# A fused Mamba and gated-FFN kernel: one more product on GpSimd, the layer norm's sums on ScalarE, and two changed instruction orders

## The reference, cut to what matters

```python
def layer(x):                                   # x: (4, 2048, 256)
    x = layernorm(x + mamba(x))
    return layernorm(x + ffn(x))

def mamba(h):                                   # 512 inner channels d, 16 states n
    x, z = split(h @ in_proj.T)
    u = silu(causal_conv4(x) + conv_b)
    dt_lo, B, C = split(u @ x_proj.T)           # 64, 16, 16 columns
    delta = softplus(dt_lo @ dt_proj.T + dt_b)
    A = -exp(A_log)
    # for each t:  h[d,n] = exp(delta[t,d]*A[d,n]) * h[d,n] + (delta[t,d]*u[t,d]) * B[t,n]
    #              y[t,d] = sum_n h[d,n] * C[t,n]
    return ((y + u * D) * silu(z)) @ out_proj.T

def ffn(x):                                     # ternary weights, hidden 1024
    h = silu(x @ w1.T * s1) * (x @ w2.T * s2)
    h = gelu(h @ h1.T * sh1); h = gelu(h @ h2.T * sh2)
    return h @ w3.T * s3
```

## Time and profile before

| | us |
|---|---|
| median of 3 runs | 3083.61 (3081.98 to 3090.67) |
| the profiled execution | 3080.23, its span 3078.4 |
| first stage's 15 full tile periods, 138.72 to 1880.20 us of the span | 1741.48 |
| DVE busy in them | 1679.70 |
| POOL busy in them | 1561.22 |
| ACT busy in them | 1322.19 |
| PE busy in them | 1512.33, at a mean granted clock of 0.92 |

### The profile page before, as it was taken

One profiled execution on the slowest core, in us unless ns is written; L12 is line 12 of the kernel. 1 busy time (PEld: TensorE's weight loads), 2 busy tenths in 40 slices (PEclk: granted clock), 3 DMA queues, 4 the chain that ended last, 5 costly groups with the idle time before them and its releaser, 6 DMA issues. The chain is left out here.

```text
span 3078.4 us, 40908 instructions
## 1 busy us (share of the span) xinstructions
PE 2735.4 (89%) x11540; PEld 1620.8 (53%) x11540; DVE 2331.5 (76%) x2785; ACT 2006.6 (65%) x3383; POOL 1705.2 (55%) x856
## 2 busy tenths in 40 slices
PE   5788998898898898888898886889999999999997
PEld 2243343343343343343343332678888888888886
DVE  5999999999999999999999999344444444444452
ACT  3777777777777777777777776555555455555442
POOL 3798898898898899898898898300000000000000
PEclk8799999999999899999999987999999999999999
DMA  7466466466476476475475466542222222222210
GB/s 254 96 186 164 124 192 169 120 192 168 120 192 164 121 196 164 117 199 152 129 198 154 127 192 204 187 146 95 69 75 89 68 82 84 79 68 89 75 42 15
DMA packets 239645, 412.04 MB, mean 134 GB/s; under 512 B 23264, under 2 KB 63456, under 8 KB 239456
## 3 DMA queue, kind: packets, MB, share of 16 engines
q1 hardware_dynamic: 175680, 297.67, 35.8%
q10 hardware_dynamic: 63776, 112.22, 11.1%
HBM read 285.55 MB, written 124.26 MB: 133 GB/s over the span
## 5 line engine op out<-in xcount | busy, mean ns | idle before, releaser
L1268 DVE TENSOR_TENSOR_SCAN h<-bank,state,db 128x512 f32<-128x512 f32 x1024 | 1252.2, 1270 | 52.8 <-POOL hc L1127 26.9
L1127 POOL TENSOR_TENSOR hc<-h,c_rows 128x1024 f32<-128x1024 f32 x512 | 1198.4, 2375 | 55.8 <-PE bank L660 41.5
L918 ACT ACTIVATE bank<-d_bc,a_neg 128x512 f32<-128x512 f32 x1024 | 691.8, 685 | 288.2 <-DVE h L1268 181.8
L1627 ACT ACTIVATE hring<-s_bank,sc 128x512 f32<-128x512 f32 x248 | 170.3, 687 | 488.6 <-PE s_bank L1560 488.3
L1560 PE MATMUL s_bank<-mid,h_r 128*128 128x512 f32 x2048 | 468.7, 390 | 4.6 <-DVEq L1654 4.6
L1252 DVE TENSOR_TENSOR db<-bank,du_bc 128x2048 f32<-128x2048 f32 x192 | 435.8, 2270 | 9.2 <-issue 7.4
L1560 PEld LDWEIGHTS s_bank<-mid,h_r 128*128 128x128 f32 x2048 | 385.7, 188 | 85.3 <-ACTq L1598 5.0
L732 PE MATMUL bank<-x_t,w 128*128 128x512 f32 x1088 | 366.0, 463 | 51.4 <-ACT ab L982 51.1
L1138 POOL TENSOR_TENSOR db<-du_bc,b_row 128x2048 f32<-128x2048 f32 x64 | 291.2, 4550 | 116.4 <-DVE h L1268 110.8
L633 PE MATMUL bank<-bc,w_spread 64*128 64x512 f32 x272 | 142.3, 533 | 203.3 <-DVE db L1252 201.3
L660 PE MATMUL bank<-hc,fold_w 128*32 128x512 f32 x2048 | 307.0, 675 | 9.1 <-DVE uz L1292 5.5
(11 more groups left out here) (145 smaller groups left out, 3706.5 us busy)
## 6 DMA issues: line engine op xcount, KB each, us to landing
ab<-ab ACTq DMA_DIRECT2D x272, 256.0 KB, 3.4
du_bc<-du_rows SPq DMA_DIRECT2D x256, 256.0 KB, 4.7
d_bc<-d_rows SPq DMA_DIRECT2D x256, 256.0 KB, 7.8
s_abr<-ab SPq DMA_DIRECT2D x120, 512.0 KB, 3.8
w<-w ACTq DMA_DIRECT2D x136, 256.0 KB, 3.4
d_rows<-sp_r SPq DMA_DIRECT2D x64, 256.0 KB, 2.1
du_rows<-sp_w SPq DMA_DIRECT2D x64, 256.0 KB, 2.2
x<-res SPq DMA_DIRECT2D x17, 512.0 KB, 9.0
```

Source lines behind the costliest of these rows:

```text
L918: act.activation(decays[DECAY_BANK[g]][:], d_bc[c % 2][:, j, :], ACT.Exp, scale=a_neg[:, g:g + 1]).then_inc(decay, 1)
L1127: pool.tensor_tensor(hc[:, k % HCSTEPS, at:at + HG], h[:, H_SLOT[k], at:at + HG], c_rows[:, q, :].unsqueeze(1).broadcast_to([P, HG, NT]), ...
L1268: dve.tensor_tensor_scan(h[:, H_SLOT[k], j, :], decays[DECAY_BANK[g]][:], db[:, k % DBSTEPS, j, :], state[:, g:g + 1], ALU.mult, ALU.add). ...
L1627: act.activation(hring[c % RING][:], p_h[m % HBANKS][:], ACT.Gelu, scale=sc[:, 2 + layer, m:m + 1]).then_inc(gelu, 1)
```

## The change

Five things are changed together.

1. **A fifth db on GpSimd.** Besides q = 3, step 10 (chunk 2, q = 2) goes to GpSimd. Steps 3, 7, 10, 11 and 15 are now GpSimd's, two of them in a row. VectorE's product and TensorE's spread for step 10 go away. Its rows of B come through one new spread at slot 13 into the softplus bank, and one new ScalarE copy at slot 14 into `b_row2`.
2. **Room for b_row2.** The ring of w1/w2 weights has three places in place of four.
3. **GpSimd's order.** The first half of hc now comes ahead of the db, the second half behind it.
4. **ScalarE's order.** A slot's decay now comes ahead of the DMA issue of that slot.
5. **The layer norm's sums.** bn_stats and bn_aggr leave VectorE. The four residual copies also write their row sums (`accum_out`), and ScalarE adds at slot 1 a 128x4 copy (the negative mean) and at slots 2 to 5 four Square activations with `accum_out`, written into the scratch `sp_e`. GpSimd's chain is one operation shorter.

```diff
+EXTRA_Q, EXTRA_C = 2, 2
+BY_POOL = [k % QN == QV or k == QN * EXTRA_C + EXTRA_Q for k in range(NK)]
+NPOOL = sum(BY_POOL)
...
+def pool_steps(k):
+
+    return k // NK * NPOOL + sum(BY_POOL[:k % NK])
...
-ABRING, W12RING = 3, 4
+ABRING, W12RING = 3, 3
@@ TensorE @@
-                        if exists(now) and g // JC % QN < QV:
+                        if exists(now) and not BY_POOL[g // JC]:
                             spread_b(now, g // JC)
...
+                        if i == ROW2_SLOT:
+                            pe.wait_ge(sp_dve, t.count(2 * KI, 2 * KI))
+                            spread_rows(p_dt, t, EXTRA_Q, row2_mm)
@@ ScalarE @@
-                act.activation(res[:, s, :], p_mm[s % 2][:, 0:DM], ACT.Copy).then_inc(out_sb, 1)
+                act.activation(res[:, s, :], p_mm[s % 2][:, 0:DM], ACT.Copy,
+                               accum_out=sums[:, s:s + 1]).then_inc(out_sb, 1)
...
+                if i == MEAN_SLOT:
+                    act.wait_ge(out_sb, t.count(SUB, OUT0))
+                    act.activation(mean4[:], sums[:], ACT.Copy, scale=-1.0 / DM).then_inc(ln_act, 1)
+                elif MEAN_SLOT < i <= MEAN_SLOT + SUB:
...
+                    act.activation(sp_e[:, s % 2 * DM:(s % 2 + 1) * DM], res[:, s, :], ACT.Square, bias=mean4[:, s:s + 1],
+                                   accum_out=squares[:, s:s + 1]).then_inc(ln_act, 1)
...
-                    if exists(t):
-                        ffn_stores(t, i)
                     now, g = at_group(t, n + EXP_LEAD)
                     if exists(now):
                         decay_of(now, g)
+                    if exists(t):
+                        ffn_stores(t, i)
...
+                        if i == ROW2_SLOT + 1:
+                            act.wait_ge(row2_mm, t.count(1, 1))
+                            act.wait_ge(db_pool, t.count(NPOOL, POOL0))
+                            act.activation(b_row2[:], p_dt[:], ACT.Copy).then_inc(row2_sb, 1)
@@ GpSimd @@
                     if n % JC == 0:
+                        done, at = at_group(t, n - JC)
+                        if exists(done):
+                            times_c(done, at // JC, range(1))
                         now, g = at_group(t, n + JC)
-                        if exists(now) and g // JC % QN == QV:
+                        if exists(now) and BY_POOL[g // JC]:
                             times_b(now, g // JC)
-                        now, g = at_group(t, n - JC)
-                        if exists(now):
-                            times_c(now, g // JC)
+                        if exists(done):
+                            times_c(done, at // JC, range(1, TURNS))
@@ VectorE @@
-                    if q < QV:
-                        dve.wait_ge(db_dve, t.count(KI * QV, QV * c + q + 1 + DVE0))
+                    if BY_POOL[k]:
+                        dve.wait_ge(db_pool, t.count(NPOOL, pool_steps(k) + 1 + POOL0))
```

More of the change, by code:

```diff
@@ L252, in mamba_stage @@
         state = sb("state", [P, NG])
-        stats = sb("stats", [P, SUB, 6])
-        mv = sb("mv", [P, SUB, 2])
+        sums, squares, mean4 = (sb(name, [P, SUB]) for name in ("sums", "squares", "mean4"))
         var4, y4 = (sb(name, [P, SUB]) for name in ("var4", "y4"))
@@ L713, in ffn_product @@
                 if which == 0:
[L714 removed]
+                    pe.wait_ge(w12_in[m % W12RING], t.count(16 * len(range(m % W12RING, KH, W12RING)), 16 * (m // W12RING + 1)))
                 before = product_before(t, e)
@@ L1045, in closing @@
                 ffn_stores(PAST, 0)
-                norm(PAST, LN_SLOT - 8)
+                for i in range(8):
+                    norm(PAST, i)
                 norm(PAST, LN_SLOT)
@@ L1117, in _, with times_c @@
             pool.sem_inc(db_pool, POOL0)
-            def times_c(t, k):
+            def times_c(t, k, turns):
                 q = k % QN
-                if k < QN:
-                    pool.wait_ge(rows_sb, t.count(ROWS, q + 2 if q else 1))
-                pool.wait_ge(folded, t.count(NK, k - HCSTEPS + 1 + FOLDED0))
-                for at in range(0, JC, HG):
+                for turn in turns:
+                    at = HG * turn
+                    if turn == 0:
+                        if k < QN:
+                            pool.wait_ge(rows_sb, t.count(ROWS, q + 2 if q else 1))
+                        pool.wait_ge(folded, t.count(NK, k - HCSTEPS + 1 + FOLDED0))
                     pool.wait_ge(scanned, t.count(NG, JC * k + at + HG + SCANNED0))
@@ L1239, in _ @@
             dve.tensor_scalar(a_neg[:], a_neg[:], -1.0, None, ALU.mult).then_inc(consts, 1)
-            dve.memset(res[:], 0.0).then_inc(out_sb, OUT0)
+            dve.memset(sums[:], 0.0).then_inc(out_sb, 1)
+            dve.memset(res[:], 0.0).then_inc(out_sb, OUT0 - 1)
             dve.memset(state[:], 0.0).then_inc(saved, SAVED0)
@@ L1292, in gate @@
                 dve.tensor_tensor(z_of(t, c), p_y[:], z_of(t, c), ALU.mult).then_inc(gated, 1)
-            STATS_SLOT, AGGR_SLOT = 1, 5
-            def norm(t, i):
-                if STATS_SLOT <= i < STATS_SLOT + SUB:
-                    s = i - STATS_SLOT
-                    if s == 0:
-                        dve.wait_ge(out_sb, t.count(SUB, OUT0))
-                    dve.bn_stats(stats[:, s, :], res[:, s, :]).then_inc(ln_dve, 1)
-                elif i == AGGR_SLOT:
-                    dve.wait_ge(ln_dve, t.count(2 * SUB, SUB))
-                    dve.sem_inc(waited, 1)
-                    for s in range(SUB):
-                        dve.bn_aggr(mv[:, s, :], stats[:, s, :]).then_inc(ln_dve, 1)
             def not_rounded(piece, raw, rounded):
@@ L1349, in tile @@
                     n = OFF + i
-                    if exists(t):
-                        norm(t, i)
                     if t is BEFORE and i == CHECK_SLOT:
@@ L1389, in _ @@
                 tile(t)
-            for i in range(AGGR_SLOT + 1):
-                norm(PAST, i)
             dve.wait_ge(counted, 1)
```

73 lines of the change are left out of this document (42 added, 31 removed).

## The result

The changed kernel takes 3122.72 us (median of 4 runs, 3120.18 to 3124.39) beside 3082.8 of the kernel before in the same comparison. The ratio is 1.0128, with a 95% interval of 1.0116 to 1.0140. The forecast of 3082 is off by 41 us, and the time lies beyond the upper end of the range, 3110.

The account below looks back on a forecast made before the run. VectorE bounds the first stage, GpSimd only 8 us a tile behind. Terms 2.5 - 1.6 + 0.6 - 1.2 - 0.4 = -0.1 us per tile, -1.6 us for 16 tiles, gave 3082 us, range 3058 to 3110.

Parts of the forecast that it names:

- The fifth db: From step 7's db to D(11), VectorE's start of step 11, GpSimd's longer queue adds 2.5 us per tile.
- The sign named for it: VectorE waits for GpSimd's db ahead of steps 10 and 11, some 6 us a tile, 90 us in 15 tiles.
- The other sign: Outside the stretch from db 7 to D(11), the period shrinks by about 2.6 us a tile.
- D(15): VectorE's start of step 15: its wait for hc 13's first half goes, -1.6 us per tile.
- db 3: At step 3, a half hc ahead of GpSimd's already late db delays VectorE's start, +0.6 us per tile.
- ScalarE's order elsewhere: Around VectorE's start of step 3, waits for decays behind stores go, -0.4 us per tile (0 to -0.9).
- The sums: Ahead of step 7's db, bn_stats leaves VectorE and a late decay gains, -1.2 us per tile (-0.4 to -1.6).
- The weight ring of three: Weight loads, issued five or more slots (9 us) ahead of use, cost nothing with three places.
- The late fold: Rival: TensorE's clock falls, GpSimd is late at db 3 in every tile; +1.6 a tile, 3109 us, chance 0.25.
- The decays as a hidden brake: Rival: no VectorE scan waits for ScalarE's decays any more; -1.5 us a tile, 3060 us, chance 0.20.
- The full gain: Rival: all work VectorE sheds counts, 5.4 us a tile, needing 4.5 of GpSimd pause; 2997 us, chance 0.07.

Follow-up runs that it names:

- e3: Changed kernel with each fold one slot earlier in TensorE's order, ahead of the spread that waits for VectorE's db; 3072.09 us, ratio 0.9962.
- e12: Changed kernel with folds one slot earlier and the fifth db at step 13 in place of step 10; 3063.43 us, ratio 0.9932.
- e4: Changed kernel with ScalarE's old order, the store's DMA issue ahead of the decay; 3120.46 us, ratio 1.0115.
- e5: Changed kernel without the fifth db and with each fold one slot earlier; both new orders and ScalarE's sums stay; 3024.76 us, ratio 0.9808.
- e11: e5 with ScalarE's old order, the store's issue ahead of the decay; 3037.01 us, ratio 0.9847.
- e8: Changed kernel with only ScalarE's sums and the weight ring of three left: no fifth db, both old orders; 3078.3 us, ratio 0.9982.
- e10: Kernel before with both new orders and early folds; bn_stats on VectorE, four dbs on GpSimd, four weight places; 3025.82 us, ratio 0.9811.
- e1: Changed kernel without the fifth db: step 10's product back on VectorE, both new orders, sums and ring kept; 3077.58 us, ratio 0.9979.
- e6: Changed kernel with TensorE computing each tile's first w1/w2 product five times, filling a gap, order unchanged; 3105.19 us, ratio 1.0067.
- e7: Kernel before with each fold one slot earlier and nothing else; 3074.57 us, ratio 0.9967.
- e9: e8 with each fold one slot earlier; 3063.93 us, ratio 0.9933.

## Why the prediction was wrong

**The fifth db (+2.5): right.** Step 7's db to D(11) grew by 2.72, from 34.26 to 36.98. The queue was counted as it ran. The stretch is full whatever else is done (36.98 in e3 too), and it costs 45 us of the time, more than the whole loss. The place is not special: at step 13 it costs 39 (e12). The sign named for it came only in part. I forecast 90 us of waits ahead of steps 10 and 11. VectorE waits 3.3 us a tile ahead of step 11, some 50 us, and in the tile shown nothing ahead of step 10. The other sign, a period that shrinks by 2.6 outside this stretch, failed outright: it grew there by 0.1.

**D(15) (-1.6): this step failed.** I wrote that counting from db 11's end GpSimd has 21.5 us of work, so that "db 15 is in time". The work was 21.4: 1017.96 - 992.74 = 25.2, less 3.8 of waits. What I left out is that three of the eight half hc in that count may start only after a fold, and that these folds stand in TensorE's queue behind a spread that waits for VectorE. I did see such a wait, but only at hc 15, and priced it only at db 3. The step measured +0.65, 2.2 more than forecast, some 36 of the 41 us. With early folds it came to -1.8 (e3), so the gain itself was real.

**db 3 (+0.6) and ScalarE's order elsewhere (-0.4): undersized.** +0.2 was forecast for D(15) to D(3) and +0.81 measured. The late fold is again the cause, here that of step 13: with early folds the stretch is 0.6 below before (e3). I took a value below the rows (0.74) because TensorE would pause less ahead of it. That did not come. GpSimd waits 2.6 us a tile for the fold before hc 15, where it waited 2.8, and the clock granted in the 11 us behind D(15) is 0.77 on average over 15 tiles, where it was 0.75. e4 shows that the -0.4 was not there in this kernel. It was in e5's (e11: 0.8 a tile), so a saving on ScalarE shows only where GpSimd doesn't set the pace.

**The sums (-1.2): met in its stretch by luck, and worth little.** D(3) to step 7's db became 1.38 shorter. But with the sums alone it is only 0.5 shorter (24.1, e8), and it is as short without them (23.8, e10) as with them (23.9, e5). It is clearly shorter than that only where D(3) itself waits for a late db 3 (23.0 in e1 and e6, 23.2 in the changed kernel), so a part of that wait seems to be won back here. In time the sums, with the ring of three, bring about 6 us of the 19 forecast alone (e8) and about 1 beside the orders (e10 beside e5). What eats their gain shows in the waits for decays: 31.6 in e8 where it was 21.2, and 18.9 in e5 where e10 has 4.5.

```profile
DVE h L1316 <- ACT bank L941: 31.6, 41, 1.5
```

Why the decays come later was not tried. In e5, without the fifth db, ScalarE works 89.8 us a tile, 1.7 more than before, and one thing that the sums add is that each `accum_out` is an instruction of its own:

```profile
L952 ACT ACTIVATION_READ_ACCUMULATOR res<-bank 128x1 f32 x56 | 10.8, 193 | 0.0
L967 ACT ACTIVATION_READ_ACCUMULATOR sp_e<-res,mean 128x1 f32 x56 | 10.5, 188 | 0.0
```

I had bounded this by one more small instruction of 0.19 on eight activations, and took 0. It is 8 x 0.19 = 1.5 us of ScalarE per tile, at the upper bound.

**The weight ring of three (0): nothing speaks against it.** It is in e5 and e8 and not in e10, and no engine waits for a transfer of weights in any of them. It was not tried alone.

**The rivals.** The late fold came nearest, 3109 for 3123: GpSimd is indeed late by waiting for folds. But it made the lower clock their cause, to which e6 gives a third, and did not see their place in TensorE's queue. It was priced at db 3 alone, and at 1.1 a tile. The decays as a hidden brake fall: early folds opened the 50 us, and e10, whose waits for decays are nearly gone (4.5), is no faster than e5 (18.9). The full gain never had its pause on GpSimd.

**What stays open.** How the rest of the folds' price divides between the spread's wait and the work piled up behind it was not separated, since e3 moves the fold ahead of both. e6 gives only a part of the clock's share, as it left some slow stretches. Nor was GpSimd's new order run alone with late folds.

## What to carry to other kernels

When work is moved ahead in one engine's queue, list what each moved instruction waits for, and follow that wait into the other engine's queue: count there not only the producer, but whatever stands in front of it and what *that* waits for. A producer that is ready should stand ahead of an instruction that waits for a third engine. Moving one group of instructions a slot earlier, at no cost in work, was here worth 10 to 15 us in the old orders (e7, and e9 beside e8) and 51 to 53 in the new ones. A reordering that measures nothing may be blocked and not worthless: try it together with the edit that its new wait points to.

## What the runs showed of the hardware

The read-out of a ScalarE accumulator is a separate record of 0.19 us behind its activation, while the activation itself keeps its length (the residual copy 366 ns before, 368 after). GpSimd and VectorE do not slow each other here. A scan takes 1264 ns in the changed kernel and 1270 before, a half hc 2375 and 2374. GpSimd was nearly as busy before as after, so that alone says little, but in the kernel before the 82 scans that ran while GpSimd was idle took 1272 ns on average, and the 807 that ran wholly beside its long instructions 1270. The Trainium skill's "Perfetto Trace Analysis", section on optimizing Scalar/DVE operations, says that the two engines share an SBUF read port, so that moving work from one to the other might not help. These rows show no such slowing. The fifth db failed to help because GpSimd's queue between steps 7 and 11 was full.

Useless products that keep TensorE busy gained 17.5 us, with the mean granted clock up from 0.935 to 0.957 and the order of the work as it was (e6).
